# Moving the recurrence's decay products and gated sum from the vector engine to GpSimd, from the third batch on

## What the kernel must compute

```python
x = x + deltanet(layernorm(x))          # gated linear recurrence, 8 heads, 2 decay rates each
x = x + layernorm(x) @ sign(W).T
x = x + attention(layernorm(x))         # causal, 16 heads of 8 features, rotary
x = x + layernorm(x) @ sign(W).T
```

```python
S = S * beta_eff + g_t * outer(k_t, v_t);   z = z * beta_eff + g_t * k_t
num = q_t @ S;   denom = q_t @ z + EPS
y_t = sum_j(num / denom * softmax(mix_t)_j)
```

## Time and profile before

| | |
|---|---|
| median of three runs | 686.31 us (685.63 to 686.48) |
| the profiled execution: span from first to last instruction | 679.2 us; its own device time is not among the numbers given |
| busy: tensor engine (PE) | 587.1 us, 86% |
| busy: vector engine (DVE) | 542.6 us, 80% |
| busy: scalar engine (ACT) | 414.9 us, 61% |
| busy: GpSimd (POOL) | 216.5 us, 32% |

### The profile page before, as it was taken

One profiled execution on the slowest core, in us unless ns is written; L12 is line 12 of the kernel. 1 busy time (PEld: TensorE's weight loads), 2 busy tenths in 40 slices (PEclk: granted clock), 3 DMA queues, 4 the chain that ended last, 5 costly groups with the idle time before them and its releaser, 6 DMA issues.

```text
span 679.2 us, 16869 instructions
## 1 busy us (share of the span) xinstructions
PE 587.1 (86%) x6352; PEld 338.2 (50%) x6352; DVE 542.6 (80%) x1547; ACT 414.9 (61%) x884; POOL 216.5 (32%) x255
## 2 busy tenths in 40 slices
PE   3686876888989899999999999999999999788995
PEld 2344534445545555555644655464646554434543
DVE  5677774889877988889899879898799877966842
ACT  2754652545777467864795767775695566346583
POOL 5261631353243251434432521535033531000000
PEclk9689787599989999999999999999999999979999
DMA  3710027000460035201540054005400433054000
GB/s 118 120 22 1 17 74 111 7 18 2 92 112 6 10 82 90 47 3 34 104 88 1 27 111 77 15 10 112 76 15 27 83 57 46 18 103 74 18 19 15
DMA packets 24914, 35.07 MB, mean 52 GB/s; under 512 B 4857, under 2 KB 22265, under 8 KB 22521
## 3 DMA queue, kind: packets, MB, share of 16 engines
q1 hardware_dynamic: 24834, 34.01, 25.4%
HBM read 22.85 MB, written 8.39 MB: 46 GB/s over the span
## 4 chain that ended last, share of the span: by engine, by line
PE 34%; DVE 27%; issue 14%; DMA 9%; POOL 7%; ACT 6%; SPq 2%; POOLq 0%; DVEq 0%; ACTq 0%
DVE mrow L1679 8%; DMA qs<-consts_bf 7%; PE ps L1215 5%; PE ps L1167 4%; PE ps L912 4%; DVE qkf L1629 3%; PE ps L1199 2%; PE ps L1196 2%; PE ps L1169 2%; PE ps L992 2%; SPq L543 2%; DVE am L1504 2%; POOL xe L624 2%; PE ps L907 2%; DMA scratch<-parts 1%
## 5 line engine op out<-in xcount | busy, mean ns | idle before, releaser
L1679 DVE TENSOR_REDUCE mrow<-ps 128x1 f32<-128x384 f32 (+3 forms) x352 | 220.5, 634 | 66.6 <-PE ps L1169 64.2
L873 ACT ACTIVATE pT<-ps 128x512 f32<-128x512 f32 (+1 forms) x330 | 173.9, 556 | 94.9 <-PE ps L1199 84.4
L1167 PE MATMUL ps<-ks,qs 72*128 72x128 bf16 (+2 forms) x384 | 101.2, 284 | 25.1 <-DVE mrow L1679 23.3
L1169 PE MATMUL ps<-ks,qs 123*128 123x128 bf16 x512 | 92.2, 226 | 6.2 <-DMA qs<-consts_bf 4.6
L1199 PE MATMUL ps<-qs,ks 75*128 75x256 bf16 (+2 forms) x384 | 93.8, 276 | 0.0
L1196 PE MATMUL ps<-qs,ks 123*128 123x128 bf16 x512 | 88.7, 223 | 5.2 <-ACT pT L873 2.4
L1215 PE MATMUL ps<-pT,va 128*32 128x512 f32 (+1 forms) x960 | 89.4, 449 | 1.8 <-DVE xk L1736 0.7
L636 POOL TENSOR_TENSOR spread<-state,cst 128x144 f32<-128x144 f32 x112 | 47.3, 444 | 121.1 <-DVE state L1533 85.1
L1167 PEld LDWEIGHTS ps<-ks,qs 72*128 72x128 bf16 x384 | 36.8, 98 | 96.7 <-DVE mrow L1679 85.8
L1196 PEld LDWEIGHTS ps<-qs,ks 123*128 123x128 bf16 x512 | 45.4, 98 | 60.9 <-ACT pT L873 26.3
L593 POOL TENSOR_TENSOR mid_rstd<-mid_ve,half 128x4 f32<-128x4 f32 x24 | 28.7, 1194 | 138.5 <-DVE mid_ve L1317 138.5
(11 more groups left out here) (209 smaller groups left out, 1091.5 us busy)
## 6 DMA issues: line engine op xcount, KB each, us to landing
ks<-scratch SPq DMA_DIRECT2D x48, 192.0 KB
scratch<-parts SPq DMA_DIRECT2D x48, 128.0 KB, 1.8
qs<-scratch SPq DMA_DIRECT2D x32, 128.0 KB
qs<-scratch SPq DMA_DIRECT2D x16, 192.0 KB
x<-x SPq DMA_DIRECT2D x8, 256.0 KB, 3.3
qs<-scratch SPq DMA_DIRECT2D x32, 64.0 KB
out<-xk SPq DMA_DIRECT2D x8, 256.0 KB, 2.3
qs<-pT SPq DMA_DIRECT2D x3, 384.0 KB, 9.2
```

Of the source, the lines that this page charges most:

```text
L873: act.activation(probs(b, g, kt)[:, c0:c0 + m, :], ps[:, score_bank(b, n), 0:m * width].rearrange("p (m n) -> p m n", n=width), ACT.Exp, s ...
L1167: pe.matmul(o[:, 0:qt * P], qs[0:K_MAX, f % RING, h, own_tile], ks[0:K_MAX, f % RING, h, 0:qt * P], start=True, stop=True, skip_group_chec ...
L1169: mm = pe.matmul(o[:, own_tile], qs[0:K_DIAG, f % RING, h, own_tile], ks[0:K_DIAG, f % RING, h, own_tile], start=True, stop=True, skip_gro ...
L1679: dve.tensor_reduce(mrow[:, qt, h0:h0 + m], ps[:, max_banks(b)[n % len(max_banks(b))], 0:m * width].rearrange("p (m k) -> p m k", k=width) ...
```

## The change

From batch 2 on (`products_aside`), three products go from the vector engine to GpSimd: the query decay products (two a batch), the key decay products (four) and the gated sum (four). They keep their tiles, semaphores and conditions. The vector engine gets one more wait: `ytmp` of a chunk is written only when the gated sum of the chunk before has been formed (`y_ready`), which is trivially so where both are on one engine. All five strings of the order are written anew. Their numbers of letters show what moves: `DVE_ORDER` has 1013 instead of 1073, `POOL_ORDER` 236 instead of 176; the others have as many as before.

```diff
 POOL_ORDER = (
-    "nnssssnssnsssssmnmsssmsssssssnnsxssmnssssmssnsmnsxsmmmmmnsnssmsmssssmasmsmnmsxmnmssmnsssssmssnammmssxmnm"
-    "ssmssmssssmmnsamsnsxmnmssnmsnsmssasmsmmssxsmmssmssmmmssasmxsssnsnmmmaxaa"
+    "nnsssssssssnnssmnsmsmssssnssnssxssssssmsssnsssmssnmsssssxssnmmmmsmssssnmsssnsmssmsssnssssammmxssssmnmsss"
+    "ssmnssssssssnsmsssammmsxsssmnmssmssnssssmmssmsssssssamnssssxmnsmssssmsnssmsssssammmssssnssssxmmsmssssnss"
+    "smmmmssassssssssnsxmmmaxaa"
 )
...
+        def products_aside(b):
+            return b >= EARLY
+
...
+                def weighted(cp):
+                    pool.wait_ge(pdec_ready, b * 2 + cp + 1)
+                    pool.wait_ge(qk_ready, b * 2 + 1)
+                    pool.tensor_tensor(qp[:, cp, :, :, :], qp[:, cp, :, :, :],
+                                       qT[:, cp * 2 * P:(cp + 1) * 2 * P].rearrange("p (k t) -> p k t", k=2)
+                                       .unsqueeze(2).broadcast_to([P, 2, J, P]), ALU.mult).then_inc(qp_ready, 1)
+
+                def keys(c):
+                    pool.wait_ge(dec_ready, b * 8 + 2 * c + 2)
+                    pool.wait_ge(ktok_ready, b + 1)
+                    pool.wait_ge(su_ps, b * 7 if c < 2 else b * 7 + 2 * c - 2)
+                    end = dec[:, c % 2, :, LB - 1].rearrange("p (h j) -> p j h", j=J)
+                    pool.tensor_tensor(kd[:, c % 2, :, :].rearrange("p j (h d) -> p j h d", d=DH),
+                                       ktok[:, c, :].rearrange("p (h d) -> p h d", d=DH).unsqueeze(1)
+                                       .broadcast_to([P, J, H, DH]),
+                                       end.unsqueeze(3).broadcast_to([P, J, H, DH]), ALU.mult).then_inc(kd_ready, 1)
+
+                def joined(c):
+                    pool.wait_ge(y_free, b * 4 + c + 1)
+                    if c == 0:
+                        pool.wait_ge(turned, b * 3 - 2)
+                    yj = ytmp[:, :, :].rearrange("p (g j i) e -> p g j (i e)", g=2, j=J)
+                    pool.tensor_tensor(ytok[:, c, :].rearrange("p (g n) -> p g n", g=2), yj[:, :, 0, :],
+                                       yj[:, :, 1, :], ALU.add).then_inc(y_ready, 1)
+
                 yield
                 decay_rows(0)
+                if products_aside(b):
+                    for cp in range(2):
+                        yield
+                        weighted(cp)
+                    yield
+                    keys(0)
                 for c in range(C):
                     if c + 1 < C:
                         yield
                         decay_rows(c + 1)
+                        if products_aside(b):
+                            yield
+                            keys(c + 1)
                     if c > 0:
+                        if products_aside(b):
+                            yield
+                            joined(c - 1)
                         yield
                         spread_state(2 * c)
                     yield
                     spread_state(2 * c + 1)
+                if products_aside(b):
+                    yield
+                    joined(C - 1)
...
-                for cp in range(2):
+                for cp in range(0 if products_aside(b) else 2):
                     yield
                     dve.wait_ge(pdec_ready, b * 2 + cp + 1)
...
+                    if b * 4 + c > 0:
+                        dve.wait_ge(y_ready, b * 4 + c)
                     dve.tensor_tensor(ytmp[:, :, :], yv[:, :, 0:DH], over_features(rec[:, :], DH),
                                       ALU.mult).then_inc(y_free, 1)
+                    if products_aside(b):
+                        return
...
-                yield
-                keys(0)
+                if not products_aside(b):
+                    yield
+                    keys(0)
...
-                        yield
-                        keys(c + 1)
+                        if not products_aside(b):
+                            yield
+                            keys(c + 1)
```

More of the change, by code:

```diff
@@ L103 @@
[L103 to L107, removed]
@@ new lines @@
+    "sasxmssaxssaxexasaxsxsxaaxasaxsxasxaxasxaaxaaaxmasxaxmxaaxassxaasxaaxaaaaaxaaaxasmaaxsaxsaxmxassxaaxasxa"
+    "xasxaaxaaaxsaxasxsaasxassaxaamxaaxsexmssxxesxssxamxssxeaxssaxsasxessxsxxsxesxsexsaxmaxaasaxsaxaxsaaxsaxa"
+    "smaxasamsaasaaaxasaxmaaaxaaaaasxmxasaxasaxaasxaxsxaxaaxaasxaxaasxmaxmaaaxsaasxmxasaxssaaxaxasxsssxesxsex"
+    "msxsaxesxexsssxaessxexssxaaxsasxsxaaxasaaxsxaxsaaxsaxaaxaasxamaxamxasaxaaaaxsaxaaaaxaasxaaaxsaxaamaxxasx"
+    "asxaaxxasxsmxsaxasasaxaaaxaaxaaxmsaxaaxsmesssxxsexssxmxesaaxsxseaxaexssaxxexssxssxmsaaxsasaxasxasxsxasxx"
@@ L110 @@
+    "aaaaaxssaxassaaxamasxaaxmxaaaxsaaxsxaaxaaxsxaaaxasaaxaamxaaaaaxsxaxaasxaxamaxassxaaaxsxaaxssaxmxmexssxss"
+    "sexamsxssxesaesxamxexsxaxssxexaxssxsxasxsaasaxssaxaxasaxssaaaaxsasaxsxasxaamxaxamxaaaxaaaxaaaaxmaxaaxaam"
+    "xaaxaaxaaxaaxaaxaaxmxamxaaxaaaxaaaxmexexxexmxexaaxxexaaxexxaxaxaaxaaxaxaxaxaaxaaaxaxxaaaaxaaaaxaxxaxxaaa"
+    "xaxxaxaxaaxxaxaxaaaaxxaaaaxaxaxaxaaxaxaaaaxaaxxaxxexexaaexaxaxexxaxaxaxaaxxaxaxxxaaxaaxaaaaeaxaaaaaaaeaa"
     "aaaaaaaaaaaaaaaaaaaaaaaaaaaaaaaeeeeee"
@@ L120 @@
+    "xaamasasassaaasasasaasasssaaaamasamaaasamaasaasammxssssseasesamsaaaaaansaaaaaaamasxaaaaaasaaaasassaaasas"
+    "asamsassssasssasaaaaaamaaamsassxmsaeasseassmamasmaasaasaanaasaaaxamasaaaaasaasaassaaaassaaasasaaaasmsaaa"
+    "ssassasamsaxmssseasmammamessssaasaaassaaaaaasxaaamaaaaaaaaaaamaaaaaaaaaamamaaaaaaamxemamaeaamaaaaaaaaaaa"
+    "aaxaaaaaaaaaaaaaaaaaaaaaaaaaaaxaaaaeaaaaaaaaaaaaaexaaaaaaaaaaaaaaaaaaaaaaaaaaaaaaaee"
 )
 DVE_ORDER = (
-    "nnnnxsssssssssnmnsmnnsssssssmsssmsmsmssssssssssssmsssssssssssssmmmmmmsssssmmsmmmsmmnsssssmsmnmsssssnssnm"
@@ L128 @@
[L128 to L132 removed]
+    "nxnnnssnnssmssmssssssssssmnmssmssmsssssnsssssssmssssssssssssmsssmmmmmsssssmmsmsmmnmmmnnmssmsssnsssssssmm"
@@ new lines @@
+    "msmmmmmmmmsssssssssssssssssssssssxsxsxsxsmsxxsxsxmxxmmxmxmxxxsxmsmxsxxsxsmmsmsxsxxxxsxmmxmsssmxssnmxxsxx"
+    "nxssxsnnssmxxmmxsssxxmxmmssxxsxxmxsssxssxmxsxxxxmmsmmmmxmxxmxxmmsxxxxxsxnxsmxmxmnmmxsxssnxsaxmxsaxmaxmax"
+    "xxxxmmxansxaxamssssxsxsmxaaxxaxsxssxsxsxxxssxsxxxxmxmxxxmxxsmmssmxmmxmssxsxsmsxnxsmxsnxmxmxxxnxxxsmxmmsx"
+    "xxxxsxaxnxxmxsaxsmxasxssxmaxmxsxsssxassxsxaxaaxamxmxaxssxssxmsxxxsssxxxxssxxmsmmmmmsmssxmssmxnxmmsxxsmxm"
+    "xnmmxxxxmxxnxsxmmxmxsmxmxsxxmxxxxxssaasxssaxmxasxxxassxssxsaxaaxnasxaxxssxssxsxxxsssxxxxxxxxmmmmxmssmsxm"
@@ L133 @@
+    "xmxmxmssxsxsxsxxmsxsxxxmxmxmmnxmnsxxxxxxsxxmxnmaaxsaaxmxsxsmxsmsxaxsxaaxsaxamxaxsnssssxmxsxxxxxssxsssxxx"
+    "xxsssxxxmxxmmsxsmsmxmxmxxsssxmxsxsxxmmxsmxxsxmxmmmxmxxxxxxsxmxaasxmasxmamxsxmmsxaxssxsxaxamxasaxxaxxssxs"
+    "ssxsxxxssssxxxxxsxsssxxxmxmmmxmmxmxxmxmmmxmxmxmxmmxxxxxmxmxmxxmxaxaxmaxaxmxmxmxmxaxaxaaaxmxaxmxxxxxxxxxx"
+    "xxxxxxxxxxxxxxxxxxxxxxxxxxxxxxxxxxaaxaaxxxxxaxxxxxxxxxxxxxxxxxaaaaaaaaaaaaaaa"
 )
 POOL_ORDER = (
-    "nnssssnssnsssssmnmsssmsssssssnnsxssmnssssmssnsmnsxsmmmmmnsnssmsmssssmasmsmnmsxmnmssmnsssssmssnammmssxmnm"
```

35 lines of the change are left out of this document (10 added, 25 removed).

## The result

The changed kernel takes 736.94 us (median of 4 runs, 729.77 to 739.85), the kernel before, beside it on the same chip, 685.97 us. The ratio is 1.0757, 95% interval [1.069, 1.0824]: 51 us slower, outside the predicted range and on the other side of it. Executions over 1.5% above the fastest of their kernel, at a lower granted clock, are left out of the ratios but not of the medians given here.

What follows compares the result with a forecast made beforehand. Neither the tensor nor the vector engine alone was taken as the bound. Relief -8.4, lateness +3.9, ports +0.3 and order 0 made -4.2 us, from 686.3 to 682.1 us; range 670 to 693, the forecast's own 675 to 685.

Steps and rivals of the forecast that it cites:

- The order written anew: All five order strings: steps move only a few places against the maxima; taken as 0, some 5 us either way.
- The relief of the vector engine, -8.4 us: Products leaving the vector engine in batches 2 to 7: 1.4 us gained per batch in saturated windows, 8.4 us in all.
- the 20.6 of the sum: Vector engine time freed by the 60 moved instructions after overlap, 20.6 us; the upper end of the gain.
- The saturated windows: Scan stretches where the vector engine has nothing left: 29.43 of 30 us and 19.81 of 20 busy.
- Rival (a): Full relief: freed vector time also shortens the maxima's back and forth with PE; 666 to 674 us, chance 10%.
- GpSimd's durations: Moved products on GpSimd: 1.16 us per query product, 0.65 per key product, 0.40 per gated sum, 39 us in all.
- The lateness at the batch's front, +3.9 us: GpSimd's queue at each batch's front: steps behind the products some 2 us late, a third on the path, 3.9 us back.
- rival (c): Slower: second decay rows and mid's power late at the batch's front, half of it on the path; 693.5 us, chance 22%.
- The ports, +0.3 us: Two-input vector work and GpSimd disturbing each other on one port; 0.3 us for 39 us more of GpSimd.
- rival (d): The lock: GpSimd's new instructions hold up two-input vector instructions, 13 us, half on the path; 688.6 us, chance 5%.
- The even trade: Rival (b): GpSimd's added work on the chain in its old proportion, -8.4 + 8.6; 686.5 us, chance 13%.
- The 7.1 us between span and time: Median run time above the traced 679.2 us span, taken as what is around it and untouched by the change.

Runs made afterwards that it cites:

- e1: The changed kernel's new orders with all three products put back on the vector engine: 756.13 us, ratio 1.0986 to the kernel before.
- e2: The kernel before with its old orders, the three products moved to GpSimd at their old places in time: 688.59 us, ratio 1.005.
- e8: e2 with each moved product cut to four columns, so GpSimd does almost nothing for it: 687.7 us, ratio 1.0024 to the kernel before.
- f2: The changed kernel with GpSimd's decay rows written by two memsets, without reads: 727.39 us, ratio 1.0595 to the kernel before.
- f3: The kernel before with GpSimd's decay rows written by two memsets, without reads: 683.73 us, ratio 0.9953.
- f4: Products moved; the new orders until the scan of batch 4, the old ones from there: 712.14 us, ratio 1.036 to the kernel before.
- f5: Products moved; the old orders until the scan of batch 4, the new ones from there: 713.89 us, ratio 1.0393 to the kernel before.
- e6: The kernel before, all work kept, plus 60 spare multiplications on GpSimd that read, at e2's places: 689.39 us, ratio 1.0045.

## Why the prediction was wrong

- **The step that failed** is "The order written anew: I find no step moved by more than a few places against the maxima, so I take 0", with its bound of 5 us either way. It measures +70 us by itself (e1) and 48 beside the move (the change less e2). The reading of the strings was nearly right: against the maxima, the steps of e2 and of the change lie less than one place apart on average on every engine, and of those over three places off (25 in all) 12 are norm steps of the vector engine, which from batch 4 on come up to 31 maxima later. Whether these matter was not tried; the 17.8 us of stretch 2 lie before them. What failed is the step from there to the cost: I had measured displacement in letters, not what it does. An engine waits in its own order, and the waits for the maxima grew by 38 and 11 us with most steps a place or less from where they had been. The bound was taken from two intervals between stores of the *same* order, which says how even a good order is and nothing on another one. The nearest evidence of a bad order was not in the trace at all, so an honest bound would have been wide, on the side of slower: the trace of one order sets no limit to what another loses.
- **The relief of the vector engine, -8.4 us**, did not come: e8 has the relief and almost none of the costs, and is 1.6 us slower than before by its ratio, at best 1.5 us faster by its interval. The vector engine's busy time fell by 16.6 us in e8, less than the 20.6 of the sum. The saturated windows are real, but PE was busy for 93 and 95% of them already, and with the orders fixed the engine's freed time turned into idle time before the reductions: 86.3 us in e8 and 86.6 in e2 against 66.6 before. Rival (a) falls with it; that the same move gave 19 us in the new orders (e1 less the change; 16 by the ratios) shows that its worth belongs to an order.
- **GpSimd's durations** were right to some 14%: predicted 1.16, 0.65 and 0.40 us, measured 1.28, 0.64 and 0.455. Its added time, 39 us, was 41.4.
- **The lateness at the batch's front, +3.9 us**, stayed untested in the change's own queue. In e2 the second decay rows stand ahead of the products, and e2 less e8 is 0.9 us (1.8 by the ratios), with the ports in it. The lateness itself came as read: in batch 5 the second decay rows end 3.8 us behind the first chunk's `dec` (392.0 and 388.2 us), where before they ended 4.2 us ahead of it (352.6 and 356.8). But e1 has the late exponents without that queue, so rival (c) named the right sign and not the cause of most of it, and its 693.5 us was far from enough.
- **The ports, +0.3 us, and rival (d)**: the excess grew by 22.5 us in the change, and by 6.5 in the old orders. The term was mis-sized by the assumption that it grows with GpSimd's busy time. It grows with what the order puts side by side: in e1 GpSimd has none of the products, and the excess is 30.8 us. In time this is 3 us in the old orders (not told apart from nothing) and, for the reads of `xe` alone, some 7 more in the new ones than in the old (f2 and f3), of 51.
- **The clock "no part of this sum"** held for the windows, where it is 1.00, and not for the kernel: 75 us more at the lower level. PE's busy time grew by 23.2 us for the same work, its idle time by 35.7 us; together they are the 58.9 us between the two profiled spans. What came first was not shown. PE had gaps before the clock fell: in the change it was busy for 3.98 of the 8 us up to 554 and for 4.49 of the 8 up to 254, and fell near the end of both. f4 and f5 tie the low stretches to the orders; but e2's tail was at 0.87 with the old order too.
- **The even trade** (b, 686.5 us) comes nearest for the move alone, 688.6 us, and by its number only: neither its relief of 8.4 us nor its cost of 8.6 is in the runs.
- **The 7.1 us between span and time** were misread as "what is around it": every execution's time lies 1.8 us above its span, and the other 5.3 us are that the traced execution was faster than the median. The forecast does not change by it, since it adds the same 7.1 to both.

What stays open: which steps of the new orders cost the time. The runs show that it is the orders (those of GpSimd's scan steps included), that both halves of the span lose and the losses add, that up to 18 us lie in batch 2's stretch, and that pairs of maxima are not it. Taking the new string on one engine and the old ones on the others was not tried, nor moving the vector engine's norm steps back, nor the change with GpSimd's scan steps in e2's order. Why the new order, made for the new placement, is this much worse can't be read from the kernel. No version was found that beats the kernel before, apart from f3, which leaves the decay rows out.

## What to carry to other kernels

Where the issue order of every engine is written out by hand or by a planner, a change of placement and a new order are two changes: measure each alone, since here the order cost 48 us beside the move, 70 without it, and the move 3. Time taken off an engine that is 80% busy and saturated in windows can be worth nothing while the order stays: here 16.6 us of it brought between 1.5 us of gain and 4.8 of loss (e8). When a diff rewrites the order and the trace can't price it, that is the widest term of the sum, not a zero.

## What the runs showed of the hardware

- GpSimd's reads stop two-input vector instructions whole: 0.35 us became 1.9, and the four instructions of batch 2 took 4.70 us together; small casts were caught as well (0.18 to 1.8 us). Of 46 stretched instructions all overlapped GpSimd. Memsets on GpSimd did not do it (excess 5.8 us with 35 us of memsets, 11.8 with 39 us of reads, 4.7 with neither).
- The stretched time does not follow GpSimd's load but what the order puts side by side: 30.8 us of excess at 215 us of GpSimd's time (e1), 11.8 at 254 (e6).
- The same 983 matmuls of the tail take PE 102.5 us at a granted clock of 0.97 and 114.6 at 0.84; executions of the kernel before took 682 to 686 us with a mean clock of 0.96 to 0.965 and 690 to 693 with 0.933 to 0.941. Such a difference in the clock goes with more time than the move alone costs.
